# Scores of two local-attention layers in blocks of 64 queries, the tables' load ahead of the weights', and a new order of steps

## The chip, the cores and the metric

The kernel runs on one core of a Trainium2 chip. The metric is the device time of one execution in microseconds; of several runs the median is taken.

## What is computed

Input x has 4 sequences of 1024 tokens with 256 channels, normalised first. Two branches work on it and are added to it: a gated sliding-window attention (16 heads), and two layers of local attention with a gated feed-forward part. The change touches the second branch. A layer of it, cut to what matters (8 heads of 64, window 128, QK_SCALE 8, HID 682):

```python
h = shift_token(x)
q, k, v = jnp.split(h @ wqkv, 3, axis=-1)         # then by heads
q = l2norm(q) * qs
k = l2norm(k) * ksc
q, k = rotary_xpos(q, k)                          # cos, sin and scale tables
sim = jnp.einsum('bhwid,bhwjd->bhwij', bq * 8, bk)  # 128 queries, 256 keys: own and previous block
mask = (i < j) | (i > j + WINDOW) | (j == -1)
attn = jax.nn.softmax(jnp.where(mask, -big, sim), axis=-1)
x = x + o @ wo
h = layernorm(shift_token(x)) * lg + lb
a, g = jnp.split(h @ w1 + b1, 2, axis=-1)
x = x + (a * gelu(g)) @ w2 + b2
```

A query sees its own position and the 128 before it, so 64 neighbouring queries see no more than 192 keys.

## The kernel before

It has two phases. `attention_phase` does the first branch and splits the layers' weights into high and low parts (projections run as three products of such parts). `layers_phase` does the two layers: eight passes (`SEQUENCES`: layer 0 of four sequences, then layer 1 of the same), each in two halves of 512 tokens. What a half does is cut into steps, listed by hand in `ORDER`. Each engine runs through the same list and does its part of each step, so the list sets the order on every engine, SyncE's and ScalarE's DMA queues included; semaphores join the engines. In each half the projections (`transpose_x`, `project_qk`, `rope`, `rope_sum`, `transpose_qk`, `project_v`) already work for the next half, beside attention and feed-forward of this one.

One unit of attention is a pair of heads on two tiles of 128 queries; a half has 8 units:

- `scores` (L1430): TensorE multiplies q and kT for 2 tiles x 2 heads, each 64 rows x 128 queries x 256 keys, into the banks `scores[a % 2][head]`. It waits for `exped` of the unit two before, which frees the bank. `scores` 1 also waits for `out` 1 of the half before, since the feed-forward's sums (`y_banks`) are `scores[1]`. VectorE adds the mask to the scores in place and takes the negative maximum (L1655).
- `softmax` (L1567): ScalarE's exponential with the row's sum. `weigh`: VectorE's reciprocal (L1663), then GpSimd's multiplication (L1305).
- `transpose` (L1438), `values` (L1453), `take_o`, `project_o` (L1352): the weights are transposed, multiplied with the values, and projected.

Other steps: `transpose_x` transposes the next half's x (L1359) into two of the three rotating banks `bank`, ScalarE copies the high part (L1520), VectorE makes the low part of actT (L1606). `project_qk` is 24 records on TensorE, then copies and squares (ScalarE), sums (VectorE, L1611) and a power (GpSimd, L1281). `rope` multiplies by the tables (VectorE L1622 and L1623, GpSimd L1287), `rope_sum` adds (VectorE L1630, L1633). `ln_stats` and `ln_apply` normalise (L1686 to L1709), `transpose_h` transposes (L1368), `up` (L1478, then L1583, L1717, L1587, L1720) and `down` (L1492) are the feed-forward part, `out` adds and stores (L1726, L1256).

SyncE's loads: `load_x` waits for the last transpose of the x before, `load_x1` for the stores of the half before, `load_tables` (L1180) for the last `rope_sum` of the half before. `load_others` does something only at the change of layer: it loads wo (L1183), the rows (L1184), w1 (L1190) and w2 (L1193, L1194) for layer 1. `load_wqkv` loads the projections' weights from ScalarE's queue, in the pass before the change.

Of the kernel before, what the change touches and what calls it, by code (L numbers as in the profile page):

```python
# [24 lines left out]
P = 128  # L25
D = 256
CT = D // P
DH = 64
SEQ = 1024
BATCH = 4  # L30
TILES = 4
# [9 lines left out]
MASKED = -1e30  # L41
# [170 lines left out]
def attention_phase(nc, kept, x, gamma, w_qkv, w_gates, b_gates, w_out, masks, identity, states, attended,  # L212
                    layer_weights, split_weights, tables_in, tables_out, q_scale, k_scale, rows_in, rows_out):

    with ExitStack() as ctx:
# [602 lines left out]
        def _(dve):  # L818
# [120 lines left out]
ORDER = [("scores", 0), ("scores", 1), ("softmax", 0), ("softmax", 1), ("weigh", 0), ("weigh", 1), ("transpose_x", 0), ("load_x", 0),  # L939
         ("scores", 2), ("transpose", 0), ("softmax", 2), ("scores", 3), ("weigh", 2), ("weigh", 3), ("load_x1", 0), ("load_others", 0),  # L940
         ("transpose", 1), ("softmax", 3), ("load_tables", 0), ("project_qk", 0), ("rope", 0), ("scores", 4), ("values", 0), ("values", 1),
         ("take_o", 0), ("transpose", 2), ("project_qk", 1), ("softmax", 4), ("scores", 5), ("weigh", 4), ("transpose", 3), ("rope_sum", 0),
         ("project_qk", 2), ("values", 2), ("softmax", 5), ("scores", 6), ("weigh", 5), ("values", 3), ("rope", 1), ("take_o", 1),
         ("transpose", 4), ("scores", 7), ("softmax", 6), ("transpose_qk", 0), ("weigh", 6), ("project_qk", 3), ("shift_keys", 0),
         ("project_o", 0), ("rope_sum", 1), ("weigh", 7), ("transpose", 5), ("values", 4), ("values", 5), ("softmax", 7), ("take_o", 2),
         ("rope", 2), ("shift_front", 0), ("transpose", 6), ("project_v", 0), ("ln_stats", 0), ("transpose_qk", 1), ("transpose", 7),
         ("ln_apply", 0), ("values", 6), ("values", 7), ("take_o", 3), ("project_v", 2), ("transpose_h", 0), ("project_o", 1), ("rope_sum", 2),
         ("up", 0), ("shift_back", 0), ("up", 1), ("up", 2), ("ln_stats", 1), ("project_v", 1), ("ln_apply", 1), ("down", 0), ("project_v", 3),
         ("up", 3), ("rope", 3), ("x1_bias", 0), ("down", 1), ("down", 2), ("transpose_h", 1), ("load_wqkv", 0), ("up", 4), ("up", 5),
# [5 lines left out]
def layers_phase(nc, kept, attended_end, states, attended, out, wqkv_in, wo_in, w1_in, w2_in, rows_in, tables_in, masks):  # L955
# [3 lines left out]
    with ExitStack() as ctx:  # L959
        def sb(name, shape, dt=F32):  # L960
            return ctx.enter_context(nc.sbuf_tensor(f"f_{name}", shape, dt))

        NU = HALVES * UNITS
        PARTS = 2
        PART = CHUNK // PARTS

        wqkv = layer_projections(kept.weights)
        wo = kept.weights[:, 2 * CT * 3 * F_INNER:KEPT_WEIGHTS].rearrange("p (t c n) -> p t c n", t=2, c=PAIRS)
# [841 lines left out]
```

## Time and profile before

| | |
|---|---|
| median of 3 runs | 2063.93 us (2059.63 to 2064.92) |
| profiled execution | 2062.13 us, span 2060.3 us |
| TensorE matmul busy | 1899.8 us, 92% |
| ScalarE busy | 1400.8 us, 68% |
| VectorE busy | 1324.1 us, 64% |
| GpSimd busy | 959.0 us, 47% |
| mean granted clock of TensorE | 0.986 |
| chain that ended last | TensorE 32%, VectorE 19%, ScalarE 9% of the span |

PE is TensorE, PEld its weight loads, DVE VectorE, ACT ScalarE, POOL GpSimd, SPq SyncE's queue. A float32 matmul stands in the trace as two records, a transpose and an fp32r product as one. A stretch's row gives its ends, its length, and for each engine busy us and the number of records, then the granted clock, the DMA engines' share and GB/s. A timeline's row gives start, length, engine, line, operation, result <- operands, shapes and the number of records merged, and in brackets the engine's idle time before it and what ended it; merged rows overlap at their edges, since the next operation starts before the last one's end. The first transposes of x (L1359) mark the halves' starts: 735.9, 817.7, and so on up to 1906.2 us.

### The profile page before, as it was taken

To read this page: it belongs to the slowest core of one execution; us is meant where nothing else is said; L and a number is where in the kernel's file an instruction comes from. 1 tells how busy PE (TensorE), PEld (TensorE's weight loads), DVE (VectorE), ACT (ScalarE), POOL (GpSimd) and SP (SyncE) were. 2 spreads that over 40 slices of the span, in tenths; PEclk is the share of its full clock that TensorE was granted. 3 is DMA by queue.
4 is the path that set the end of the run, shared out by engine and by line. 5 is a ranking of instruction groups with operands and counts; after the bars stand their busy time and mean duration, and the time that the engine had idled before them with its cause. 6 is when DMAs were issued, how large, how long until landed. Compare 5 with 4: busy or idle time off the path is not lost.

```text
span 2060.3 us, 42560 instructions
## 1 busy us (share of the span) xinstructions
PE 1899.8 (92%) x15184; PEld 1575.3 (76%) x15184; DVE 1324.1 (64%) x4117; ACT 1400.8 (68%) x3933; POOL 959.0 (47%) x1311
## 2 busy tenths in 40 slices
PE   5999999999999789999999999997999999999998
PEld 3777787777777668778788787795877878878777
DVE  4543544444443467777778777775777877877775
ACT  4886977778678465775766757756576575675763
POOL 1532442334234463654736526545264562664732
PEclk9999999999999899999999999998999999999999
DMA  3231322313225411010110110304101011010110
GB/s 126 86 101 43 97 82 78 96 58 89 82 75 161 149 39 36 14 42 11 45 45 12 44 42 15 103 7 158 33 29 52 21 45 55 16 47 22 34 35 26
DMA packets 121493, 121.10 MB, mean 59 GB/s; under 512 B 27188, under 2 KB 100804, under 8 KB 121284
## 3 DMA queue, kind: packets, MB, share of 16 engines
q1 hardware_dynamic: 118116, 112.10, 17.0%
q10 hardware_dynamic: 3168, 6.29, 0.9%
q8 instruction: 122, 2.00, 0.4%
q14 instruction: 87, 0.71, 0.1%
HBM read 72.72 MB, written 37.25 MB: 53 GB/s over the span
## 4 chain that ended last, share of the span: by engine, by line
PE 32%; DVE 19%; ACT 9%; issue 2%; POOL 2%; SPq 1%; DMA 1%; DVEq 0%; ACTq 0%; POOLq 0%
PE f_bank L1352 11%; PE f_scores L1492 4%; ACT f_prob L1567 4%; PE f_scores L1430 4%; DVE f_u L1720 4%; PE f_bank L1478 4%; PE f_bank L1438 3%; DVE f_gu L1717 2%; PE f_o_bank L1453 2%; ACT f_u L1587 2%; DVE y_tok L1703 2%; PE f_bank L1403 2%; DVE y_tok L1709 1%; POOL f_prob L1305 1%; DVE f_sin_part L1623 1%
## 5 line engine op out<-in xcount | busy, mean ns | idle before, releaser
L1305 POOL TENSOR_SCALAR f_prob<-f_prob,f_row_inv 128x256 f32<-128x256 f32 x512 | 263.1, 533 | 331.0 <-DVE f_row_inv L1663 331.0
L568 POOL TENSOR_SCALAR a_prob<-a_prob,a_row_inv,a_gate 128x128 f32<-128x128 f32 x512 | 224.6, 455 | 409.8 <-DVE a_row_inv L898 409.8
L1352 PE MATMUL f_bank<-weights,f_actT 128*128 128x512 f32 x1152 | 305.6, 410 | 1.6 <-DVE f_actT L1606 1.6
L1478 PE MATMUL f_bank<-f_hT,f_w 128*128 128x256 f32 x2112 | 276.5, 286 | 7.7 <-DVE f_gu L1717 7.7
L1478 PEld LDWEIGHTS f_bank<-f_hT,f_w 128*128 128x128 f32 x2112 | 262.1, 190 | 14.3 <-DVE f_gu L1717 10.8
L1567 ACT ACTIVATE f_prob<-f_scores,f_neg_max 128x256 f32<-128x256 f32 x512 | 235.9, 488 | 41.8 <-DVE f_neg_max L1655 40.8
L1352 PEld LDWEIGHTS f_bank<-weights,f_actT 128*128 128x128 f32 x1152 | 211.2, 193 | 51.2 <-ACT f_probT L1514 5.1
L1281 POOL TENSOR_TENSOR f_norm<-f_norm,f_minus_half 128x16 f32<-128x16 f32 x64 | 197.5, 3085 | 24.8 <-DVE f_norm L1615 22.4
L1655 DVE CUSTOM_DVE_ANT_0 f_scores<-f_scores,f_mask 128x256 f32<-128x256 f32 x512 | 199.8, 455 | 13.5 <-PE f_scores L1430 13.4
L1587 ACT ACTIVATE f_u<-f_gu 128x256 fp32r<-128x256 f32 x192 | 80.2, 418 | 180.8 <-DVE f_gu L1717 180.8
L797 ACT ACTIVATE a_prob<-a_scores,a_neg_max 128x128 f32<-128x128 f32 x512 | 179.5, 390 | 30.2 <-DVE a_neg_max L889 28.9
L1287 POOL TENSOR_TENSOR f_qk_tok<-f_qk_tok,tables 128x512 f32<-128x512 f32 x128 | 161.6, 1283 | 71.5 <-DVE f_sin_part L1623 71.5
L591 PE MATMUL a_bank<-a_xT,weights 128*128 128x512 f32 x768 | 191.4, 400 | 0.0
L1438 PE MATMUL f_bank<-ident,f_prob 128*128 128x128 f32 x1024 | 147.8, 280 | 41.9 <-POOL f_prob L1305 15.3
L1720 DVE TENSOR_TENSOR f_u<-f_gu,f_u 128x256 fp32r<-128x256 f32 x192 | 125.6, 654 | 92.9 <-ACT f_u L1587 92.9
L1514 ACT ACTIVATE f_probT<-f_bank 128x512 f32<-128x512 f32 x256 | 146.4, 613 | 54.5 <-PE f_bank L1438 53.5
L591 PEld LDWEIGHTS a_bank<-a_xT,weights 128*128 128x128 f32 x768 | 142.6, 189 | 35.6 <-issue 2.2
L1438 PEld LDWEIGHTS f_bank<-ident,f_prob 128*128 128x128 f32 x1024 | 109.7, 141 | 78.2 <-issue 36.7
L1492 PE MATMUL f_scores<-f_w,f_u 128*128 128x256 f32 (+1 forms) x1152 | 164.2, 286 | 0.0
L1430 PE MATMUL f_scores<-f_kT,f_q 64*128 64x256 f32 x1024 | 147.5, 405 | 17.5 <-ACT f_prob L1567 16.8
L1492 PEld LDWEIGHTS f_scores<-f_w,f_u 128*128 128x128 f32 (+1 forms) x1152 | 148.2, 189 | 6.1 <-issue 2.5
L889 DVE CUSTOM_DVE_ANT_0 a_scores<-a_scores,a_mask 128x128 f32<-128x128 f32 x512 | 129.9, 325 | 34.0 <-PE a_scores L659 34.0
(128 smaller groups left out, 3844.2 us busy)
## 6 DMA issues: line engine op xcount, KB each, us to landing
split_weights<-a_hi_lo SPq DMA_DIRECT2D x16, 512.0 KB, 2.8
x_next<-states SPq DMA_DIRECT2D x32, 256.0 KB, 3.1
tables<-scaled_tables SPq DMA_DIRECT2D x16, 512.0 KB, 6.0
f_x<-states SPq DMA_DIRECT2D x16, 512.0 KB, 5.2
split_weights<-a_hi_lo SPq DMA_DIRECT2D x12, 682.0 KB, 4.0
weights<-split_weights ACTq DMA_DIRECT2D x6, 1024.0 KB, 9.7
f_w<-split_weights SPq DMA_DIRECT2D x4, 1280.0 KB, 9.9
a_x_tok<-in_x SPq DMA_DIRECT2D x8, 512.0 KB, 4.4
```

What stands on the lines that cost most here:

```text
L568: last = nc.gpsimd.tensor_scalar(part, part, row_inv[:, a % 2, head, t:t + 1], gate[:, half, t, h:h + 1], ALU.mult, ALU.mult)
L591: last = nc.tensor.matmul(out, lhs(c, a), rhs(c, b), start=(i == 0), stop=(i == len(order) - 1))
L1281: nc.gpsimd.tensor_tensor(n, n, minus_half[:], ALU.pow).then_inc(norm_ready.sem, 1)
L1305: last = nc.gpsimd.tensor_scalar(part, part, row_inv[:, a % 2, head, t:t + 1], 1.0, ALU.mult, ALU.mult)
L1352: last = nc.tensor.matmul(out, lhs(c, a), rhs(c, b), start=(i == 0), stop=(i == len(order) - 1))
L1430: mm = nc.tensor.matmul(scores[a % 2][head][:, t, :], q[rows, pair, col:col + P], kT[rows, pair, col:col + 2 * P], start=True, stop=True)
L1438: last = nc.tensor.transpose(out[:, j * P:(j + 1) * P], prob[:, a % 2, head, j // 2, (j % 2) * P:(j % 2 + 1) * P], ident[:])
L1478: mm = nc.tensor.matmul(out[:, which * PART:(which + 1) * PART], w1[:, wp, c, col:col + P], hT[:, hp, c, columns_of(a // FH)], start=(i == ...
L1492: mm = nc.tensor.matmul(y_banks[a // FH % PARTS][:, t, :], u[0:m, a % (2 * TILES), up, t * P:(t + 1) * P], w2[0:m, wp, j, :], start=(j == ...
L1567: last = nc.scalar.activation(prob[:, a % 2, head, t, :], scores[a % 2][head][:, t, :], ACT.Exp, bias=neg_max[:, a % 2, head, t:t + 1], sc ...
L1655: last = nc.vector.tensor_tensor_reduce(out=sc, in0=sc, in1=mask[:, min(half * TILES + tile + t, 1)], scale=-1.0, scalar=3e38, op0=ALU.add ...
L1720: nc.vector.tensor_tensor(u[0:m, a % (2 * TILES), LO, :], gu[0:m, a % 2, :], u[0:m, a % (2 * TILES), HI, :].bitcast(F32), ALU.subtract).th ...
```

## The change

1. A `scores` step takes each tile's 128 queries in two blocks of 64 with 192 keys each: 8 matmuls of 64 rows x 64 queries x 192 keys in place of 4 of 64 x 128 x 256. Head 0 and 1 lie in rows 0-63 and 64-127 of the array, block 0 and 1 in columns 0-63 and 64-127. The quarter of the result that isn't written now (block 0's last 64 keys, block 1's first 64) is cleared once, by four memsets at the head of VectorE's part, and TensorE waits for them once before its first scores.
2. Since the mask is added in place over what is left there, its sign and that of q change: the q tables are multiplied by -8, the layers' mask is +1e30 where masked, and VectorE's operation has scale 1.0.
3. `ORDER` is new: `transpose_x` stands between `scores` 0 and 1 and ahead of `softmax` 0; on SyncE the order of the loads is `load_x1`, `load_tables`, `load_x`, `load_others` where it was `load_x`, `load_x1`, `load_others`, `load_tables`; `load_wqkv` stands later; `values`, `transpose_qk`, `rope` 2, `up` and `down` steps are moved.

```diff
-ORDER = [("scores", 0), ("scores", 1), ("softmax", 0), ("softmax", 1), ("weigh", 0), ("weigh", 1), ("transpose_x", 0), ("load_x", 0),
-         ("scores", 2), ("transpose", 0), ("softmax", 2), ("scores", 3), ("weigh", 2), ("weigh", 3), ("load_x1", 0), ("load_others", 0),
-         ("transpose", 1), ("softmax", 3), ("load_tables", 0), ("project_qk", 0), ("rope", 0), ("scores", 4), ("values", 0), ("values", 1),
-         ("take_o", 0), ("transpose", 2), ("project_qk", 1), ("softmax", 4), ("scores", 5), ("weigh", 4), ("transpose", 3), ("rope_sum", 0),
-         ("project_qk", 2), ("values", 2), ("softmax", 5), ("scores", 6), ("weigh", 5), ("values", 3), ("rope", 1), ("take_o", 1),
-         ("transpose", 4), ("scores", 7), ("softmax", 6), ("transpose_qk", 0), ("weigh", 6), ("project_qk", 3), ("shift_keys", 0),
-         ("project_o", 0), ("rope_sum", 1), ("weigh", 7), ("transpose", 5), ("values", 4), ("values", 5), ("softmax", 7), ("take_o", 2),
-         ("rope", 2), ("shift_front", 0), ("transpose", 6), ("project_v", 0), ("ln_stats", 0), ("transpose_qk", 1), ("transpose", 7),
-         ("ln_apply", 0), ("values", 6), ("values", 7), ("take_o", 3), ("project_v", 2), ("transpose_h", 0), ("project_o", 1), ("rope_sum", 2),
-         ("up", 0), ("shift_back", 0), ("up", 1), ("up", 2), ("ln_stats", 1), ("project_v", 1), ("ln_apply", 1), ("down", 0), ("project_v", 3),
-         ("up", 3), ("rope", 3), ("x1_bias", 0), ("down", 1), ("down", 2), ("transpose_h", 1), ("load_wqkv", 0), ("up", 4), ("up", 5),
-         ("down", 3), ("add_attended", 0), ("up", 6), ("up", 7), ("up", 8), ("up", 9), ("rope_sum", 3), ("down", 4), ("transpose_qk", 2),
-         ("down", 5), ("up", 10), ("down", 6), ("up", 11), ("down", 7), ("down", 8), ("transpose_qk", 3), ("out", 0), ("down", 9), ("down", 10),
-         ("down", 11), ("out", 1)]
+ORDER = [("scores", 0), ("transpose_x", 0), ("softmax", 0), ("scores", 1), ("weigh", 0), ("load_x1", 0), ("weigh", 1), ("softmax", 1),
+         ("scores", 2), ("transpose", 0), ("scores", 3), ("weigh", 2), ("softmax", 2), ("load_tables", 0), ("transpose", 1), ("softmax", 3),
+         ("values", 0), ("weigh", 3), ("project_qk", 0), ("values", 1), ("rope", 0), ("load_x", 0), ("scores", 4), ("take_o", 0),
+         ("transpose", 2), ("project_qk", 1), ("scores", 5), ("weigh", 4), ("softmax", 4), ("rope_sum", 0), ("load_others", 0), ("transpose", 3),
+         ("values", 2), ("scores", 6), ("weigh", 5), ("softmax", 5), ("project_qk", 2), ("rope", 1), ("values", 3), ("take_o", 1), ("scores", 7),
+         ("transpose", 4), ("softmax", 6), ("weigh", 6), ("project_qk", 3), ("project_o", 0), ("rope_sum", 1), ("weigh", 7), ("transpose", 5),
+         ("values", 4), ("softmax", 7), ("values", 5), ("take_o", 2), ("transpose", 6), ("project_v", 0), ("transpose_qk", 0),
+         ("shift_front", 0), ("values", 6), ("transpose", 7), ("ln_stats", 0), ("shift_keys", 0), ("ln_apply", 0), ("transpose_qk", 1),
+         ("rope", 2), ("transpose_h", 0), ("values", 7), ("take_o", 3), ("project_v", 2), ("rope_sum", 2), ("up", 0), ("project_o", 1),
+         ("up", 1), ("up", 2), ("project_v", 1), ("shift_back", 0), ("down", 0), ("down", 1), ("ln_stats", 1), ("ln_apply", 1), ("down", 2),
+         ("up", 3), ("project_v", 3), ("rope", 3), ("transpose_h", 1), ("up", 4), ("up", 5), ("down", 3), ("up", 6), ("x1_bias", 0), ("up", 7),
+         ("up", 8), ("down", 4), ("rope_sum", 3), ("down", 5), ("down", 6), ("load_wqkv", 0), ("transpose_qk", 2), ("up", 9), ("up", 10),
+         ("down", 7), ("up", 11), ("down", 8), ("down", 9), ("transpose_qk", 3), ("add_attended", 0), ("out", 0), ("down", 10), ("down", 11),
+         ("out", 1)]
...
+        BLOCK = P // 2
+        KEYS = F_WINDOW + BLOCK
...
+            pe.wait_ge(scores_zeroed, 1)
...
-                            col = (tile + t) * P
-                            for head in (0, 1):
-                                rows = slice(DH * head, DH * (head + 1))
-                                mm = nc.tensor.matmul(scores[a % 2][head][:, t, :], q[rows, pair, col:col + P],
-                                                      kT[rows, pair, col:col + 2 * P], start=True, stop=True)
+                            for b in (0, 1):
+                                col, first = (tile + t) * P + b * BLOCK, b * BLOCK
+                                for head in (0, 1):
+                                    rows = slice(DH * head, DH * (head + 1))
+                                    mm = nc.tensor.matmul(scores[a % 2][head][first:first + BLOCK, t, first:first + KEYS],
+                                                          q[rows, pair, col:col + BLOCK], kT[rows, pair, col:col + KEYS], start=True, stop=True)
...
+            dve.memset(scores[0][0][:], 0.0)
+            dve.memset(scores[0][1][:], 0.0)
+            dve.memset(scores[1][0][:], 0.0)
+            dve.memset(scores[1][1][:], 0.0).then_inc(scores_zeroed, 1)
...
-                                last = nc.vector.tensor_tensor_reduce(out=sc, in0=sc, in1=mask[:, min(half * TILES + tile + t, 1)], scale=-1.0,
+                                last = nc.vector.tensor_tensor_reduce(out=sc, in0=sc, in1=mask[:, min(half * TILES + tile + t, 1)], scale=1.0,
...
-    other = np.where((distance >= 0) & (distance <= window), 0.0, MASKED)
-    first = np.where(first_block & (place < window), MASKED, other)
+    masked = MASKED if window < P else -MASKED
+    other = np.where((distance >= 0) & (distance <= window), 0.0, masked)
+    first = np.where(first_block & (place < window), masked, other)
...
-    tables = np.stack([f(8) * cos * scale, f(8) * sin * scale, cos / scale, sin / scale], axis=1)
+    tables = np.stack([f(-8) * cos * scale, f(-8) * sin * scale, cos / scale, sin / scale], axis=1)
```

## Rows read from the trace of the kernel before

**Rows 1.** Busy time by stretch: two ordinary halves and the change of layer.

```profile
core 0: us, PE busy (x) PEld busy (x) DVE busy (x) ACT busy (x) POOL busy (x), PEclk, DMA share, GB/s
1311.30:1392.80 81.50, 78.42 (x599) 66.41 (x597) 62.27 (x167) 54.88 (x142) 42.46 (x47) 1.00 0.10 30
1392.80:1489.80 97.00, 82.25 (x582) 69.11 (x580) 63.36 (x167) 54.92 (x142) 44.59 (x48) 0.91 0.28 92
1489.80:1572.50 82.70, 78.81 (x598) 66.43 (x596) 63.48 (x167) 54.88 (x142) 44.84 (x48) 1.00 0.11 36
```

**Rows 2.** Waits of TensorE: us in total, times, longest.

```profile
PE f_scores L1430 <- ACT f_prob L1567: 16.8, 16, 2.1
...
PE f_bank L1438 <- DVE f_actT L1606: 12.1, 15, 0.8
...
PE f_bank L1438 <- DVE f_norm L1611: 10.6, 1, 10.6
...
PE f_bank L1478 <- DVE f_gu L1717: 7.7, 15, 0.6
```

**Rows 3.** Timeline of TensorE, one scores step; the middle two are from narrow windows.

```profile
1328.63 1.13 PE L1430 MATMUL f_scores<-f_kT,f_q 64*128 64x256 f32 x8
...
1328.95 0.60 PE L1430 MATMUL f_scores<-f_kT,f_q 64*128 64x256 f32 x4
...
1329.17 0.60 PE L1430 MATMUL f_scores<-f_kT,f_q 64*128 64x256 f32 x4
...
1329.70 1.09 PE L1438 MATMUL f_bank<-ident,f_prob 128*128 128x128 f32 x8
```

**Rows 4.** Timeline of TensorE in the attention phase: two scores steps on quarters.

```profile
533.82 1.98 PE L659 MATMUL a_scores<-a_kT,a_q 64*64 64x128 f32 x64
535.73 4.47 PE L591 MATMUL a_bank<-a_wv,a_xT 128*128 128x512 f32 x18
```

**Rows 5.** Timeline of VectorE at the start of the layers.

```profile
690.00 1.29 DVE L1606 TENSOR_TENSOR f_actT<-f_bank,f_actT 128x512 fp32r<-128x512 f32 x2 [2.49 <-ACT f_actT L1520]
```

**Rows 6.** Timeline of TensorE at the start of a half.

```profile
1311.28 1.09 PE L1359 MATMUL f_bank<-ident,x_next 128*128 128x128 f32 x8
1313.39 1.14 PE L1430 MATMUL f_scores<-f_kT,f_q 64*128 64x256 f32 x8 [1.02 <-ACT f_prob L1567]
1314.97 0.63 PE L1438 MATMUL f_bank<-ident,f_prob 128*128 128x128 f32 x4 [0.45 <-POOL f_prob L1305]
1316.42 0.66 PE L1438 MATMUL f_bank<-ident,f_prob 128*128 128x128 f32 x4 [0.82 <-DVE f_actT L1606]
```

**Rows 7.** Timeline of VectorE there.

```profile
1309.47 0.69 DVE L1726 TENSOR_TENSOR f_x<-f_scores,f_x 128x512 f32<-128x512 f32 x1 [1.27 <-PE f_scores L1492]
1310.50 0.43 DVE L1655 CUSTOM_DVE_ANT_0 f_scores<-f_scores,f_mask 128x256 f32<-128x256 f32 x1 [0.34 <-PE f_scores L1430]
...
1313.52 0.17 DVE L1663 RECIPROCAL f_row_inv<-f_row_sum 128x4 f32<-128x4 f32 x1
```

**Rows 8.** ScalarE there: the timeline, then the chain of waits.

```profile
1308.28 1.28 ACT L1567 ACT_TABLE_LOAD   x1
...
1311.40 3.75 ACT f_prob L1567 x16
```

**Rows 9.** Timeline of GpSimd: the power of one project_qk step.

```profile
1336.98 2.91 POOL L1281 TENSOR_TENSOR f_norm<-f_norm,f_minus_half 128x16 f32<-128x16 f32 x1
```

**Rows 10.** The change of layer: SyncE's timeline, chain, TensorE's timeline, a stretch.

```profile
1411.33 0.36 SPq L1180 DMA_DIRECT2D tables<-scaled_tables  x1
...
1411.33 6.66 DMA tables<-scaled_tables
...
1422.04 1.12 PE L1438 MATMUL f_bank<-ident,f_prob 128*128 128x128 f32 x4 [10.59 <-DVE f_norm L1611]
1422.81 5.28 PE L1352 MATMUL f_bank<-weights,f_actT 128*128 128x512 f32 x12
...
1415.00:1420.00 5.00, 0.00 (x0) 0.00 (x0) 1.99 (x7) 0.00 (x0) 0.62 (x1) 0.50 0.31 99
```

More of the change, by code:

```diff
@@ L1081, in layers_phase @@
         x2_stored = count("x2_stored", {"out": 1}, unit=16, credit=1)
-        pad_zeroed = sem("pad_zeroed")
+        pad_zeroed, scores_zeroed = sem("pad_zeroed"), sem("scores_zeroed")
         consts_loaded = sem("consts_loaded")
```

## The prediction

> **What bounds the kernel now.** The attention phase (the first 689 us) keeps its code, so I read the two layers, which run from 689 us to the end. Their work repeats 16 times, once for each half of each of the eight sequences. I read first the busy time by stretch. A half of layer 0 takes 81.5 us and TensorE is busy for 78.4 of them; a half of layer 1 takes 82.7 us with 78.8. VectorE has 62 to 63 us of work, ScalarE 55, GpSimd 43 to 45 [rows 1]. TensorE's work bounds a half, and the other engines matter where they make it wait. One stretch stands out: the half at the change of layer takes 97.0 us, 14.3 more than its neighbour in layer 1, at a mean granted clock of 0.91 [rows 1].
>
> Second, who made TensorE wait. The 16 waits of scores for the exponentials cost 16.8 us, the 15 of transposes for the low part of actT 12.1, and a single one for f_norm 10.6 [rows 2]. Third, the timelines at the places of these waits: one at the start of each half and one at the change of layer.
>
> **The scores on quarters of the array.** A scores step before is 4 matmuls, 8 records of 256 columns, and the next step starts 1.07 us after it (1329.70 less 1328.63). Its pairs of records start 0.22 us apart (1328.95 and 1329.17), so four pairs make 0.86 and 0.21 lie at the ends of the step [rows 3]. After, a step is 8 matmuls, 16 records of 192 columns, on four quarters. The nearest operation is the attention phase's own: 64 rows on 64 columns, 64 records of 128 columns in two steps, 1.91 us from its start to the next work (535.73 less 533.82) [rows 4]. That is 0.12 us for each group of four; scaled by 192/128 a group takes 0.18 and a new step 0.72 us. This is one bound, a gain of 0.35. The other keeps the 0.21 at the ends whole and scales the four groups by 192/256: 0.65 and 0.21 are 0.86, a gain of 0.21. I take a gain of 0.25, near the second, because the ends of the step stay. There are 128 steps, so TensorE has 32 us less to do (27 to 45), 2.0 us in each half.
>
> Here a rule speaks against the change. The attention phase's records of 128 columns take 1.91/64 = 0.030 us each [rows 4], so a record carries no large fixed price when four run side by side. The Trainium skill, TensorEngine Tiling (Array Packing), Instruction Overhead, gives each matmul some 60 cycles of overhead; with 8 more records in a step that would be an estimated 0.2 us at the full clock, which would leave nearly nothing of the 0.25. By that rule, the sum below would be about 25 us higher; the row disagrees with it, so I don't use it.
>
> The additions of the mask keep their count and shape, only the sign moves to the tables, so they cost what they did. The parts of the scores' banks that no matmul writes any more hold large numbers; their time isn't shown by any row, and I take it as none, since the same instructions read the same number of elements.
>
> **The four memsets.** They stand first on VectorE in the layers, which has to make the low part of actT at 690.0 us, for which it waited 2.49 us [rows 5]. No row shows a memset of these banks by VectorE. By the 0.65 us of each of the two operations in that row (512 columns) four take 2.6 us, and by half of that 1.3; they can start once the engine is in the layers, about 688.5. So TensorE's first projection comes 0 to 1.1 us later. I take 1.0; the lower bound is none.
>
> **The start of a half.** Before, scores 0 and 1 end at 1311.28, the transposes of x follow, and TensorE idles 1.02 us before scores 2, 0.45 before the first four transposes of the weights, 0.82 before the next four: 2.3 us [rows 6]. VectorE subtracts nothing until out 1 has run (1309.47); then two steps of scores last from 1310.50 to 1313.52, 1.5 each [rows 7]. ScalarE loads the table of the exponential at 1308.28 for 1.28 us, under its wait, and then makes 16 exponentials in a row in 3.75, 1.9 for a step [rows 8].
> After, transpose_x stands ahead of softmax 0 and of scores 1. The load stands directly before the first exponential, behind the copies of the step before it [rows 8]; I take it that it stays there. So ScalarE first waits for the transposed x (about 1310.5), copies it twice (0.6 each), loads the table, and begins the exponentials at 1312.9 and not at 1311.4. VectorE does scores 0 to 1311.8, the low part of actT to 1313.1 (two of 0.65), scores 1 to 1314.7, and only then the reciprocal of step 0. GpSimd has the first head at 1315.9, and the transposes of step 0 start at 1316.0 where they began at 1314.97. TensorE idles there some 1 us longer than before, in two waits (before scores 2, and before transpose 0), while the wait for the bank behind actT (0.82) goes. From there I follow the two orders by these durations up to the end of transpose 2: both come out near 1325.9. So four of the eight shortened scores, 1.0 us of the 2.0, are spent at the start of the half.
>
> **The rest of a half.** The other four give 1.0 us. The new order puts rope 2 behind ln_apply 0, which takes two operations (1.3 us) out of the way to transpose_h 0, and it has at most three up steps in a row, where four ended in a wait for VectorE [rows 2] of 0.5 us in a half. Against that, transpose 4 needs weigh 4, which stands on GpSimd behind the power of project_qk 1: one such power is 2.9 us [rows 9], and by my working weigh 4 ends 0.2 us ahead of its use. That is the tightest place; QK 3 also waits some 0.4 for its bank. I take 0.3 us net for the order and give a half 1.3 us (bounds: a loss of 0.5, a gain of 3.0). Over 15 halves that is 19.5 us. The last half has no projections to cover the same chain, and I give it 0.5.
>
> **The change of layer.** Before, SyncE issues the other weights first and the tables only at 1411.33; they land 6.66 us later, and VectorE's rope, and all behind it, waits. TensorE idles 10.59 us, and in that pause the granted clock falls to 0.50, its lower level of 1.2 GHz, so that the next projection's 12 records take 5.28 us [rows 10]. The excess of that half, 14.3 us, is both. After, load_tables stands right behind load_x1 and ahead of load_x and load_others. It is issued near 1396.5 and lands by 1403 with that 6.66, while rope 0 needs it some 15 us after the half's start, about 1407. Who is passed: the load of x for the next half (needed a whole half later) and the other weights. These are issued about 1 us later than before, over 15 us; the first use of wo is 30 us into the half and of w1 45 us. So I take all 14.3 (bounds: 10.6 and 14.5). At the other places the tables were ahead of their use already. The first projections of layer 1 are asked for later, about 20 us ahead of their use; no row makes me charge for it.
>
> **The sum**, against the profiled execution's 2062.1 us (span 2060.3 and 1.8 around it): less 19.5, less 0.5, less 14.3, plus 1.0 gives 2028.8. The median of the runs is 1.8 above the profiled one, so 2030.6; I say **2031**.
>
> **The rivals.**
> - The whole of the gain arrives. The 2.0 us of every half and the start's idle of 2.3 both go, at least by half: 16 x (2.0 + 0.6) + 14.3 - 1 = 55, a time of 2009. For it: TensorE is the fullest engine. Against it: at the start of a half the chain over VectorE, ScalarE and GpSimd has no slack, and two more engines' work is now in it.
> - The chain takes it all. If the start costs 2 us and the rest is bound by VectorE (its row of work in the up steps has hardly a gap), only the change of layer is left: 2064 - 14 + 1 = 2051.
> - The tables still come late, behind x1 and the stores: 2031 + 14 = 2045. Against it, the queue's rows show the wait as issues of the other weights.
> - Slower: weigh 4 falls behind one more power on GpSimd (2.9 us) on top of 1.5 us of ScalarE's copies and table at the start. That is 4.4 us lost in each half against 2.0 saved: 15 x 2.4 = 36 against 14.3, a time of 2087. It decides from a loss of 2.95 us in a half (2.0 + 14.3/15).
> - It doesn't do what it says: the four quarters run two by two. Then a step has eight turns of 0.16 and is 1.5 us, 0.43 more, 128 times: plus 55 on the work, near 2090. The attention phase's 0.12 us for each four speaks against it.
>
> **Chances.** The forecast (2020 to 2040) has 0.58; the whole gain 0.16; the chain takes it all 0.14; tables late 0.04; slower by the chain 0.05; quarters two by two 0.01; and 0.02 for little net effect. For 8 times in 10 the range goes from 2012 to 2050. A measurement of this kernel tells 0.3% (6 us) from no change. Faster by more than that: 0.91; within: 0.03; slower: 0.06.
>
> **What would show it.** Scores steps of 0.80 to 0.86 us from start to next work; a wait before scores 2 of about 3 us and one before transpose 0, but none behind actT; table load behind the copies of actT; no 10 us wait and a clock of 1.00 in the half at the change of layer, which then takes as long as its neighbours; halves of about 80.3 us. I am wrong if scores steps stay above 0.95 us, if GpSimd's weigh 4 or 6 makes TensorE wait in each half, or if w1 or wo comes late.

## The result

The changed kernel takes 2074.8 us (median of 5 runs, 2072.0 to 2078.3) where the kernel before takes 2064.1 on the same chip: a ratio of 1.0059, 95% interval 1.0048 to 1.0070. It is slower by some 11 us; 2031 was forecast, and the range ended at 2050.

| | before | after |
|---|---|---|
| median of the runs | 2064.1 | 2074.8 |
| profiled execution, its span | 2062.1, 2060.3 | 2076.4, 2074.6 |
| mean granted clock of TensorE | 0.986 | 0.971 |
| a half of layer 0 | 81.5 to 82.5 | 83.3 to 84.2 |
| a half of layer 1 | 82.7 to 83.7 | 84.1 to 85.4 |
| the half at the change of layer | 97.0 | 84.5 |

(A half is taken from the start of its transposes of x to the next half's, in the profiled executions.) So the change of layer came out nearly as forecast, and the other halves, forecast to be 1.3 us shorter each, are 1.7 longer on average (84.2 against 82.6). Two halves and one stretch of 2.5 us at the start of the first, in after (the columns are those of [rows 1]):

```profile
1324.50:1407.80 83.30, 78.17 (x664) 66.05 (x660) 61.48 (x164) 55.03 (x142) 44.63 (x47) 0.98 0.10 32
1407.80:1492.30 84.50, 77.94 (x648) 65.27 (x644) 62.64 (x165) 55.07 (x142) 46.88 (x48) 0.98 0.31 104
1330.00:1332.50 2.50, 2.50 (x23) 1.75 (x16) 1.16 (x6) 1.64 (x7) 2.50 (x6) 0.50 1.07 387
```

GpSimd has 2 us more in the half, though it does the same work [rows 1], and a clock of 0.50 appears where it was 1.00. The clock falls so at each of the 14 starts from the second half on, in some only behind scores 2. Who made TensorE wait, in after (us in total, times, longest), beside [rows 2]:

```profile
PE f_scores L1434 <- ACT f_prob L1571: 51.2, 25, 3.2
PE f_bank L1442 <- POOL f_prob L1307: 28.7, 48, 1.2
```

The waits of scores for the exponentials grew from 16.8 us to 51.2. In before the waits of transposes for GpSimd were 15.3.

**The start of a half.** TensorE's timeline in after, to be read against [rows 6]:

```profile
1323.64 0.88 PE L1434 MATMUL f_scores<-f_kT,f_q 64*64 64x192 f32 x16
1324.45 1.09 PE L1361 MATMUL f_bank<-ident,x_next 128*128 128x128 f32 x8
1325.48 0.88 PE L1434 MATMUL f_scores<-f_kT,f_q 64*64 64x192 f32 x16
1329.53 1.56 PE L1434 MATMUL f_scores<-f_kT,f_q 64*64 64x192 f32 x16 [3.17 <-ACT f_prob L1571]
1331.02 1.78 PE L1442 MATMUL f_bank<-ident,f_prob 128*128 128x128 f32 x8
```

and ScalarE's, beside [rows 8]:

```profile
1325.15 1.08 ACT L1524 ACTIVATE f_actT<-f_bank 128x512 fp32r<-128x512 f32 x2 [2.30 <-PE f_bank L1361]
1326.25 1.28 ACT L1571 ACT_TABLE_LOAD   x1
1327.55 0.47 ACT L1571 ACTIVATE f_prob<-f_scores,f_neg_max 128x256 f32<-128x256 f32 x1
```

Scores 0 lasts 0.81 us from its start to the next (1324.45 less 1323.64), as forecast. ScalarE copies, loads its table, and begins the exponentials 3.9 us after scores 0 begins. TensorE waits 3.17 us. What comes next was in no line of the forecast: the granted clock falls to 0.50, the lower level (1.2 GHz), and scores 2 and the transposes behind it take 1.49 and 1.71 us to the next step, where the full clock (2.4 GHz) needs 0.81 and some 1.0.

**The middle of a half.** GpSimd's timeline in after, without a gap from its first power to weigh 7:

```profile
1341.03 3.28 POOL L1283 TENSOR_TENSOR f_norm<-f_norm,f_minus_half 128x16 f32<-128x16 f32 x1 [0.70 <-DVE f_norm L1623]
1344.28 2.51 POOL L1289 TENSOR_TENSOR f_qk_tok<-f_qk_tok,tables 128x512 f32<-128x512 f32 x2
1346.90 2.90 POOL L1283 TENSOR_TENSOR f_norm<-f_norm,f_minus_half 128x16 f32<-128x16 f32 x1
1349.78 5.70 POOL L1307 TENSOR_SCALAR f_prob<-f_prob,f_row_inv 128x256 f32<-128x256 f32 x8
1355.46 2.91 POOL L1283 TENSOR_TENSOR f_norm<-f_norm,f_minus_half 128x16 f32<-128x16 f32 x1
1358.34 2.52 POOL L1289 TENSOR_TENSOR f_qk_tok<-f_qk_tok,tables 128x512 f32<-128x512 f32 x2
1360.84 3.77 POOL L1307 TENSOR_SCALAR f_prob<-f_prob,f_row_inv 128x256 f32<-128x256 f32 x4
1364.57 2.91 POOL L1283 TENSOR_TENSOR f_norm<-f_norm,f_minus_half 128x16 f32<-128x16 f32 x1
1367.47 1.97 POOL L1307 TENSOR_SCALAR f_prob<-f_prob,f_row_inv 128x256 f32<-128x256 f32 x4
```

Weigh 6 (1360.84) takes 3.77 us for four multiplications that take 1.84 elsewhere. TensorE waits for it:

```profile
1364.75 0.63 PE L1442 MATMUL f_bank<-ident,f_prob 128*128 128x128 f32 x4 [1.24 <-POOL f_prob L1307]
```

Why it is slow is seen in narrow windows: two of the multiplications of weigh 6, and what VectorE does at that time (rope_sum 1):

```profile
1361.29 1.44 POOL L1307 TENSOR_SCALAR f_prob<-f_prob,f_row_inv 128x256 f32<-128x256 f32 x1
1362.71 1.44 POOL L1307 TENSOR_SCALAR f_prob<-f_prob,f_row_inv 128x256 f32<-128x256 f32 x1
```

```profile
1360.89 1.50 DVE L1638 TENSOR_TENSOR f_qk_tok<-f_qk_tok,f_sin_part 128x1024 f32<-128x1024 f32 x1 [0.48 <-POOL f_qk_tok L1289]
1362.50 1.31 DVE L1641 TENSOR_TENSOR f_qk_tok<-f_qk_tok,f_norm 128x1024 f32<-128x1024 f32 x1
```

Each of the two starts while one of VectorE's operations on two tiles is running, takes 1.44 us instead of 0.46, and ends 0.34 us behind it (1362.73 against 1362.39, 1364.15 against 1363.81). The whole trace of after has 45 multiplications that start so, three in a half, and every one ends 0.34 to 0.35 us behind VectorE's operation; before has 15, one in a half. The Trainium skill, SBUF — State Buffer, Who interferes with whom, says that a VectorE instruction with two SBUF inputs and a GpSimd one that reads SBUF share a port which one of them holds for its whole instruction, while the other is blocked. By that rule weigh 6 should lose about what is left of the two operations when its multiplications start, 1.10 us each, and the rows agree: 1.93 us in all.

Last, the page's chain that ended last, before and after (shares of the span by engine):

```profile
PE 32%; DVE 19%; ACT 9%; issue 2%; POOL 2%; SPq 1%; DMA 1%; DVEq 0%; ACTq 0%; POOLq 0%
```

```profile
PE 35%; POOL 16%; DVE 7%; ACT 5%; issue 3%; DMA 0%; SPq 0%; ACTq 0%; DVEq 0%; POOLq 0%
```

GpSimd went from 2% to 16%. The chain reaches back to the start of the layers alone (688.7 us in before), which is two thirds of the span. So TensorE, which the forecast made the bound of a half, had about half of it in before, and VectorE more than a quarter.

### The profile page after: what moved, and what is told of

The parts are those of the page before. It is cut to its first block, busy times and chain, and to the rows that moved or that the text cites. A ratio compares the mean times of both kernels' runs of the same rounds, so it can differ in the third digit from the quotient of the medians.

```text
span 2074.6 us, 44612 instructions
## 1 busy us (share of the span) xinstructions
PE 1899.2 (92%) x16208; PEld 1572.8 (76%) x16208; DVE 1301.6 (63%) x4121; ACT 1406.7 (68%) x3933; POOL 985.8 (48%) x1311
## 3 DMA queue, kind: packets, MB, share of 16 engines
q1 hardware_dynamic: 118116, 112.10, 16.8%
## 4 chain that ended last, share of the span: by engine, by line
PE 35%; POOL 16%; DVE 7%; ACT 5%; issue 3%; DMA 0%; SPq 0%; ACTq 0%; DVEq 0%; POOLq 0%
PE f_bank L1482 9%; PE f_bank L1354 9%; POOL f_prob L1307 8%; PE f_scores L1496 6%; POOL f_norm L1283 5%; PE f_bank L1442 3%; PE f_scores L1434 3%; POOL f_qk_tok L1289 2%; PE f_o_bank L1457 2%; DVE f_u L1728 2%; ACT f_prob L1571 2%; PE f_bank L1405 1%; DVE y_tok L1717 1%; ACT L1571 1%; PE f_bank L1370 1%
## 5 line engine op out<-in xcount | busy, mean ns | idle before, releaser
L1307 POOL TENSOR_SCALAR f_prob<-f_prob,f_row_inv 128x256 f32<-128x256 f32 x512 | 294.4, 596 | 336.8 <-DVE f_row_inv L1671 335.8
L1354 PE MATMUL f_bank<-weights,f_actT 128*128 128x512 f32 x1152 | 300.5, 406 | 2.3 <-DVE f_actT L1614 2.3
L1283 POOL TENSOR_TENSOR f_norm<-f_norm,f_minus_half 128x16 f32<-128x16 f32 x64 | 191.9, 2999 | 27.3 <-DVE f_norm L1623 25.6
L1442 PE MATMUL f_bank<-ident,f_prob 128*128 128x128 f32 x1024 | 162.5, 302 | 29.2 <-POOL f_prob L1307 28.7
L1442 PEld LDWEIGHTS f_bank<-ident,f_prob 128*128 128x128 f32 x1024 | 122.2, 153 | 73.7 <-issue 47.3
L1434 PE MATMUL f_scores<-f_kT,f_q 64*64 64x192 f32 x2048 | 128.8, 373 | 52.9 <-ACT f_prob L1571 51.2
L1587 ACT ACTIVATE f_gu<-f_bank,f_rows 128x256 f32<-128x256 f32 x192 | 90.3, 471 | 100.5 <-PE f_bank L1482 99.1
```

The lines of the kernel that those rows point to most:

```text
L1283: nc.gpsimd.tensor_tensor(n, n, minus_half[:], ALU.pow).then_inc(norm_ready.sem, 1)
L1307: last = nc.gpsimd.tensor_scalar(part, part, row_inv[:, a % 2, head, t:t + 1], 1.0, ALU.mult, ALU.mult)
L1354: last = nc.tensor.matmul(out, lhs(c, a), rhs(c, b), start=(i == 0), stop=(i == len(order) - 1))
L1434: mm = nc.tensor.matmul(scores[a % 2][head][first:first + BLOCK, t, first:first + KEYS], q[rows, pair, col:col + BLOCK], kT[rows, pair, co ...
L1442: last = nc.tensor.transpose(out[:, j * P:(j + 1) * P], prob[:, a % 2, head, j // 2, (j % 2) * P:(j % 2 + 1) * P], ident[:])
```

## The experiments

Times are medians; ratios are to the kernel before on the same chip, with 95% intervals. "Old" and "new" name the order of the steps.

### The parts by themselves, and TensorE's clock

**e1**: the old order, with the quarters (scores, mask, memsets); ORDER is that of the kernel before.

```diff
+                            for b in (0, 1):
+                                col, first = (tile + t) * P + b * BLOCK, b * BLOCK
...
+            dve.memset(scores[0][0][:], 0.0)
```

> The kernel before with the quarters, the changed signs and the four memsets, but the old order of steps. Theory A (the new order costs what the quarters give: a wait of 3.2 us at each half's start, after which the clock falls, and a full GpSimd): here the time falls by 10 to 25 us, to about 2046; the scores step is 0.81 us from start to next work, the wait before scores 2 stays under 2 us, the granted clock stays 1.00 there, the change of layer still costs its 14 us. Theory B (the quarters themselves cost: more records, a change of the array's shape at each step): no gain or a loss, 2064 or more, and the work behind a scores step starts later than before.

Measured: 2074.7, ratio 1.0053 (1.0036 to 1.0070). The shorter scores alone make the kernel slower. The time is theory B's, but its reason isn't: a scores step is 0.81 us, and what stands behind it starts no later. Two halves of e1 and a stretch in the second:

```profile
898.50:981.00 82.50, 77.12 (x648) 64.08 (x644) 63.85 (x165) 54.62 (x142) 43.50 (x47) 1.00 0.10 33
1063.60:1147.40 83.80, 79.29 (x649) 66.05 (x645) 62.53 (x165) 54.70 (x142) 43.45 (x47) 0.96 0.11 33
1068.10:1074.90 6.80, 5.98 (x33) 4.61 (x33) 4.50 (x19) 5.47 (x19) 3.23 (x8) 0.50 0.45 148
```

and the same half of the kernel before as the first:

```profile
899.70:982.20 82.50, 78.05 (x582) 65.58 (x580) 63.20 (x167) 54.82 (x142) 43.42 (x47) 1.00 0.10 33
```

Where the clock stays at 1.00 the half takes 82.5 us with either shape: TensorE is busy for 0.9 less and waits 0.9 longer. Read step by step from the half's start, scores 3 to 7 each start 0.22 to 0.28 us later than before, and the step behind each starts when it did, within 0.03 us. In the other half of e1 the clock is at 0.50 for 6.8 us. Around its start TensorE waited three times, the third time as the clock fell:

```profile
1065.90 0.88 PE L1434 MATMUL f_scores<-f_kT,f_q 64*64 64x192 f32 x16 [1.23 <-ACT f_prob L1571]
1067.49 0.63 PE L1442 MATMUL f_bank<-ident,f_prob 128*128 128x128 f32 x4 [0.70 <-POOL f_prob L1307]
1068.94 1.12 PE L1442 MATMUL f_bank<-ident,f_prob 128*128 128x128 f32 x4 [0.82 <-DVE f_actT L1614]
```

2.75 us of waits, where before had 2.29 [rows 6] and kept its clock in every ordinary half. These same waits stand in nearly every start of e1, and a fall follows at 7 of 14.

**e2**: the new order, loads included, with the scores as before.

```diff
-ORDER = [("scores", 0), ("scores", 1), ("softmax", 0), ...
+ORDER = [("scores", 0), ("transpose_x", 0), ("softmax", 0), ("scores", 1), ...
```

> The kernel before with the new order of steps alone; scores stay 64 x 128 x 256. Theory A: the change of layer gives back 12 to 14 us, and each of the other halves loses about 2 to 3.5 us; the sum is 2080 to 2095. TensorE's wait before scores 2 is about 2.7 us. If the clock falls there too, transposes 0 take 1.8 us in place of 1.0. Theory B: faster than before, about 2050.

Measured: 2083.1, 1.0097 (1.0070 to 1.0123). The new order alone is slower by 20 us in spite of its tables. Its halves take 83.4 to 85.6, the one at the change of layer 86.2, TensorE waits 2.92 us ahead of scores 2.

**e3**: the kernel before with the loads moved alone.

```diff
-("transpose_x", 0), ("load_x", 0), ... ("load_x1", 0), ("load_others", 0), ... ("load_tables", 0),
+("transpose_x", 0), ... ("load_x1", 0), ("load_tables", 0), ("load_x", 0), ("load_others", 0), ...
```

> The kernel before with only SyncE's loads moved: load_x1, load_tables, load_x, load_others. All theories: the half at the change of layer takes 83 to 84.5 us in place of 97.0, other halves are unchanged within 0.2 us, and the time is 2050 to 2052. If w1 or wo came late for it, there would be a new wait before the projections of o or the up steps in that half.

Measured: 2052.4, 0.9951 (0.9935 to 0.9967). This part does what it was forecast to do. The half at the change of layer takes 83.7 us, and the clock stays at 1.00 from the first half to the last:

```profile
745.00:1970.00 1225.00, 1163.62 (x8708) 977.47 (x8706) 942.82 (x2430) 813.79 (x2102) 659.98 (x710) 1.00 0.13 40
```

**e4**: e3 with the quarters.

> The quarters of e1 and the loads of e3 with the old order otherwise. Theory A: the two gains add, about 2033 (2025 to 2042). Theory B: no better than e3, 2050 or more.

Measured: 2063.2, 1.0002 (0.9992 to 1.0011): the quarters take 10.8 us of e3's gain away, as theory B had it. Two of its halves:

```profile
983.30:1065.30 82.00, 78.38 (x664) 65.82 (x660) 62.05 (x165) 54.69 (x142) 42.61 (x47) 0.98 0.09 30
1065.30:1149.40 84.10, 79.55 (x649) 66.27 (x645) 62.62 (x165) 54.83 (x142) 43.60 (x47) 0.96 0.10 33
```

The short fall (mean clock 0.98) is made up for within the half (e3 has 82.1 there), the longer one (0.96) costs 1.6 us (82.5 in e3).

**e8**: e4 with the matmuls of scores 1 issued twice.

```diff
+                        for again in range(2 if s == 1 else 1):
```

> e4 (quarters, old order, tables first; 2063.2) with the matmuls of scores 1 done twice, 0.65 us more work for TensorE in a wait of 1.23 us. If e4's 10.8 us above e3 (which has the long scores and no fall of the clock) are the clock's: it stays 1.00 in nearly all halves, and the time is e3's, about 2052 (2049 to 2055), no better, since the shorter scores save nothing in a half whose clock stayed up (82.5 us with and without). If the quarters cost by themselves: 2063 or more.

Measured: 2053.7, 0.9956 (0.9942 to 0.9970), which is e3's time. The repeat fills TensorE's wait (0.58 us ahead of scores 2, where e4 has 1.23), computes nothing new, and 9.5 us come back. So what the quarters cost in the old order is the clock, and the time of the scores themselves is worth nothing there. The clock isn't fully held: it falls for a short time at 5 of e8's 14 starts, where e4 has 8, and that with waits of 2.11 us in all, less than the 2.29 of before. The length of these waits alone doesn't decide it.

### The start of a half in the new order

**e5**: the changed kernel with the matmuls of scores 1 three times over. **e6**: the changed kernel with one exponential of a single column ahead of the copies of x, so that the table is loaded before them. **e7**: both.

```diff
+                    if kind == "transpose_x":
+                        nc.scalar.activation(early[:], ident[:, 0:1], ACT.Exp)
```

> The changed kernel, but the eight matmuls of scores 1 are done three times over (the same result), 1.3 us more work for TensorE in each half, laid into its wait of 3.17 us before scores 2; only the clock can gain by it. If the fall of the clock after that wait costs what the trace shows (scores 2 and the transposes 0 at half speed, about 1.4 us a half in 15 halves): the wait falls to about 1.9 us, the clock stays 1.00 at the halves' starts, and the time falls by 12 to 22 us, to about 2057. If the fall of the clock has another cause, or what it delays is hidden: no gain, 2072 to 2078.

> The changed kernel, but ScalarE makes one exponential of a 128 x 1 column before it waits for the transposed x, so that the table (1.28 us) is loaded in that wait. If the table's load on the chain is what makes the start long: softmax 0 begins some 1.2 us earlier, as soon as VectorE has the first maxima and the copies of actT are done, the wait before scores 2 falls from 3.17 to about 2, the clock stays up, and the time falls to about 2055 (2045 to 2065). If VectorE's order (scores 1 ahead of the reciprocal) holds the start anyway: 2070 or more.

> e5 and e6 together. By the first theory of each, no more than e6 gains plus a few us, about 2052, since both keep the clock up and only e6 shortens the chain. If the rest of a half is held by GpSimd and VectorE, no better than 2048.

Measured: e5 2071.3, 1.0042 (1.0024 to 1.0060); e6 2072.7, 1.0051 (1.0031 to 1.0070); e7 2070.4, 1.0038 (1.0024 to 1.0051). In e5 the wait of 3.17 becomes 1.87 and the clock falls at every second start only. In e6 the wait is split into 1.75 and 1.40 and the clock still falls. In e7 it is 0.45 and 1.84. Each is within 4.4 us of the changed kernel, and the gain of 12 to 22 us that e5's first theory asked for didn't come. The mean granted clock of e5 is 0.985, nearly the 0.986 of before, where the changed kernel has 0.971; so the clock is not where most of its loss lies. The wait of 1.24 us for weigh 6 is in e5 as it was.

### GpSimd's queue

**e9**: the changed kernel with GpSimd's powers taken of 2 of their 16 columns (most of the normalisation of q and k is left out). **e10**: the same in the kernel before.

```diff
-                nc.gpsimd.tensor_tensor(n, n, minus_half[:], ALU.pow).then_inc(norm_ready.sem, 1)
+                nc.gpsimd.tensor_tensor(n[:, 0:2], n[:, 0:2], minus_half[:, 0:2], ALU.pow).then_inc(norm_ready.sem, 1)
```

> The changed kernel with GpSimd's powers (the reciprocal roots of q's and k's sums of squares) taken of 2 of their 16 columns, so that GpSimd spends some 0.4 us instead of 2.9 us on each; the other columns of the normalisation stay sums of squares, so part of the normalisation is left out. GpSimd's theory: in the changed order GpSimd is busy from the first power to weigh 7 without a gap, and TensorE's transposes 6 wait 1.24 us for weigh 6; with the four powers of a half 10 us shorter this wait is gone and what stands behind the powers on VectorE starts earlier, so that a half comes down by 1 us or more: below 2060 us. The rival, that ScalarE's and VectorE's chain with the clock at the start sets a half: the wait of transposes 6 goes, and the time stays within 4 us of the changed kernel's 2075.

> The same short powers in the kernel before, as the control, with the same part of the normalisation left out. GpSimd's theory: GpSimd has 2% of the chain that ended last in the kernel before, so the gain is smaller than the changed kernel's by at least 8 us: 2055 to 2064. The rival: powers are on the chain of both orders alike, and both kernels gain the same.

Measured: e9 2041.9, 0.9895 (0.9875 to 0.9915), 33 us under the changed kernel; e10 2050.0, 0.9930 (0.9904 to 0.9955), 13.5 us under the kernel before. The difference of the gains, some 19 us, is put down to GpSimd's queue in the new order. e10's own number was a miss: an engine with 2% of the chain that ended last was still worth 13.5 us.

**e11**: the changed kernel with one step moved.

```diff
-         ("values", 2), ("scores", 6), ("weigh", 5), ("softmax", 5), ("project_qk", 2), ("rope", 1), ("values", 3), ...
-         ("transpose", 4), ("softmax", 6), ("weigh", 6), ("project_qk", 3), ("project_o", 0), ("rope_sum", 1), ...
+         ("values", 2), ("scores", 6), ("weigh", 5), ("softmax", 5), ("project_qk", 2), ("values", 3), ...
+         ("transpose", 4), ("softmax", 6), ("weigh", 6), ("rope", 1), ("project_qk", 3), ("project_o", 0), ("rope_sum", 1), ...
```

> The changed kernel with one step moved: rope 1 (two multiplications on GpSimd and what feeds them) behind weigh 6 instead of ahead of it, so that weigh 6 doesn't stand behind it and doesn't run beside VectorE's two-input sums. GpSimd's theory: the 1.24 us wait of transposes 6 goes and a half is 1 to 1.5 us shorter: 2055 to 2065. The clock's theory: the clock at the start of a half holds the half, and the middle of it is caught up anyway: within 4 us of 2075.

Measured: 2051.0, 0.9937 (0.9913 to 0.9960). One step moved takes 24 us off the changed kernel, more than was expected. In the profiled executions the ordinary halves average 83.0 us, where the changed kernel has 84.2. GpSimd's timeline in e11:

```profile
1330.93 3.28 POOL L1283 TENSOR_TENSOR f_norm<-f_norm,f_minus_half 128x16 f32<-128x16 f32 x1 [0.71 <-DVE f_norm L1623]
1334.18 2.52 POOL L1289 TENSOR_TENSOR f_qk_tok<-f_qk_tok,tables 128x512 f32<-128x512 f32 x2
1336.81 2.90 POOL L1283 TENSOR_TENSOR f_norm<-f_norm,f_minus_half 128x16 f32<-128x16 f32 x1
1339.70 4.67 POOL L1307 TENSOR_SCALAR f_prob<-f_prob,f_row_inv 128x256 f32<-128x256 f32 x8
1344.34 2.91 POOL L1283 TENSOR_TENSOR f_norm<-f_norm,f_minus_half 128x16 f32<-128x16 f32 x1
1347.24 2.35 POOL L1307 TENSOR_SCALAR f_prob<-f_prob,f_row_inv 128x256 f32<-128x256 f32 x4
1349.56 2.52 POOL L1289 TENSOR_TENSOR f_qk_tok<-f_qk_tok,tables 128x512 f32<-128x512 f32 x2
1352.05 2.90 POOL L1283 TENSOR_TENSOR f_norm<-f_norm,f_minus_half 128x16 f32<-128x16 f32 x1
1354.97 1.84 POOL L1307 TENSOR_SCALAR f_prob<-f_prob,f_row_inv 128x256 f32<-128x256 f32 x4
```

From the first power to the end of weigh 7 it is 25.88 us, where the changed kernel has 28.41; weigh 6 takes 2.35 and not 3.77. These 2.53 us are in the multiplications. But weigh 6 also no longer stands behind rope 1 (2.52 us), so it ends 4.9 us earlier after the first power (18.7 for 23.6), half by the shorter multiplications and half by its place. e11 doesn't tell which half is needed to end the wait of 1.24. The waits of TensorE for weighed scores fall from 28.7 us to 5.1, while those at the starts, and the falls of the clock, are still all there:

```profile
PE f_scores L1434 <- ACT f_prob L1571: 51.1, 25, 3.2
...
PE f_bank L1442 <- POOL f_prob L1307: 5.1, 11, 0.6
```

**e12**: e11 with the matmuls of scores 1 three times over.

> The same, and the matmuls of scores 1 issued three times over, so that TensorE waits shorter for the first exponentials and its clock falls at fewer starts. If both the clock and GpSimd's queue cost time, each by itself, 2048 to 2058, below the kernel before. If neither does, within 4 us of 2071, what the threefold scores 1 gave alone.

Measured: 2042.9, 0.9896 (0.9874 to 0.9918), the fastest kernel that computes all of it: 21 us below the kernel before, and below the expected range. The repeat takes 8.1 us off e11, where it took 3.5 off the changed kernel. That the clock counts for more once GpSimd's queue is out of the way would fit, but the two gains differ by less than their intervals allow to tell.

### What the shape of the scores is worth in the new order

**e13**: e11 with the scores as before. **e14**: e13 with scores 1 issued twice.

> The changed order with rope 1 behind weigh 6, and the scores as before: 128 queries with 256 keys. If the shape of the scores saves nothing and only lowers the clock, this is at or under e11's 2051: 2043 to 2051. If the shorter scores bring part of their 0.25 us a step once GpSimd no longer holds the half, this is slower than e11: 2055 to 2075.

> The same with the matmuls of scores 1 issued twice over, which fills TensorE's wait at the start of a half as the threefold short ones did in e12 (2043). If the shape of the scores is worth nothing: 2040 to 2047. If it is worth its 2 us a half: 2060 to 2075.

Measured: e13 2060.5, 0.9982 (0.9971 to 0.9993); e14 2053.1, 0.9947 (0.9929 to 0.9965). e13 falls into the second case of its expectation, e14 between the two. The shape is worth something here, though not its 2 us a half: 9.4 us between e13 and e11, 10.2 between e14 and e12. It was already worth 8.3 us in the new order with rope 1 at its first place (e2 against the changed kernel). The chains of the pages of e11, e2 and e1:

```profile
PE 47%; ACT 9%; DVE 7%; POOL 1%; issue 1%; DMA 0%; SPq 0%; ACTq 0%; DVEq 0%; POOLq 0%
```

```profile
PE 36%; POOL 15%; DVE 6%; ACT 5%; issue 4%; DMA 0%; SPq 0%; ACTq 0%; DVEq 0%; POOLq 0%
```

```profile
PE 30%; DVE 20%; ACT 10%; POOL 3%; issue 3%; SPq 1%; DMA 0%; DVEq 0%; ACTq 0%; POOLq 0%
```

Of the two thirds of the span that the chain covers, TensorE has most in e11 and less than half in e1. That fits a shape that is worth something in the one and nothing in the other. But e2 has hardly more than the old order, and the quarters gain there as well, so the share doesn't give the price. The runs together:

| order of the steps | scores as before | on quarters |
|---|---|---|
| old | 2064 (before) | 2074.7 (e1) |
| old, tables first | 2052.4 (e3) | 2063.2 (e4) |
| old, tables first, scores 1 twice | | 2053.7 (e8) |
| new | 2083.1 (e2) | 2074.8 (changed kernel) |
| new, rope 1 later | 2060.5 (e13) | 2051.0 (e11) |
| new, rope 1 later, scores 1 repeated | 2053.1 (e14) | 2042.9 (e12) |

## Why the prediction was wrong

The table can be walked from the kernel before to the changed one: 2064, less some 12 for the tables (e3), plus 8 for the rest of the new order with rope 1 later (e13), less 9 for the quarters (e11), plus 24 for rope 1's place (the changed kernel). Such a walk ends at 2075 whatever its steps mean. What the steps are worth shows in other pairs: rope 1's place 22.6 us with the full scores (e2 against e13), the quarters less 8 to 10 in the new order but plus 11 in the old one.

Set against the forecast's terms, the largest part of the 44 us between 2031 and 2075 is GpSimd's. The order was to give 0.3 us in each of 15 halves, 4.5 us, and rope 1's place took 24: 28 us. The shorter scores less what they spend at the start were to give 1.0 us in each half, 15 us, and give about 1 (9 less 8). The change of layer gave 10 to 13 us where 14.3 were forecast.

So three steps failed: every weigh step was taken at the duration of an undisturbed one, shorter scores were taken as time saved because TensorE was taken for the bound, and the wait at the start of a half was charged without the lower clock behind it.

Step by step:

- **"TensorE's work bounds a half."** This failed. The busy share (78.4 of 81.5 us) was read as the bound. But a TensorE whose every step comes just in time is as busy as one that others wait for. e1 and e8 show it: 0.9 us less work in a half and the same 82.5 us, and no gain over e3 where the clock is nearly held. The chain that ended last, with VectorE at 19% beside TensorE's 32%, was a warning and wasn't weighed.
- **A scores step is 0.25 us shorter.** Right (0.81 to 0.82 from start to next, on 1.07). The rule of the Trainium skill, TensorEngine Tiling (Array Packing), Instruction Overhead, on some 60 cycles for each matmul, which the prediction set aside, isn't borne out: by it the step would have gained nearly nothing, and it gained 0.26 us. But 32 us less work for TensorE is worth only 8 to 10 us with the new order and costs 11 with the old one.
- **The memsets, 1.0 us.** Four of 0.48 us; TensorE's first projection waits 2.25 us instead of 1.57, so 0.7 us.
- **The start of a half.** The hand-worked chain was right to some tenths: copies, table, exponentials, a wait of "about 3 us" (3.17), none behind actT. What failed is the step from that wait to its price. The prediction had, in [rows 10], a pause of TensorE followed by a clock of 0.50, and charged the start of a half for the idle time alone. The clock fell at each of the 14 starts, and in the one shown scores 2 and the transposes ran at half speed. Filling the wait gives back 3.5 us in the changed kernel (e5) and 8.1 in e11 (e12).
- **"The tightest place"**: GpSimd was the right engine, the place was weigh 6 in place of weigh 4, and the error lies in a duration: a weigh step, for which the prediction shows no row, was taken at 1.84 us everywhere. The kernel before already shows it at 2.79 where it runs beside rope_sum:

```profile
1334.21 2.79 POOL L1305 TENSOR_SCALAR f_prob<-f_prob,f_row_inv 128x256 f32<-128x256 f32 x4
...
1339.87 1.83 POOL L1305 TENSOR_SCALAR f_prob<-f_prob,f_row_inv 128x256 f32<-128x256 f32 x4
```

  Against the margin of 0.2 us that was stated for weigh 4 this 0.95 is large; in the new order it is 1.93 for weigh 6 and 2.0 for weigh 4 and 5 together. The net gain of 0.3 us from the order was in truth a loss of some 1.6 us a half (24 us over 15 halves). The last section of the prediction named "weigh 4 or 6 makes TensorE wait in each half" as the sign of its error, and that is the row that came.
- **The change of layer, 14.3 us.** Right in kind, somewhat too large: that half is 12.5 us shorter in after and 13.3 in e3, and e3's runs are 10.4 faster.
- **The rivals.** "Slower by the chain" had the engine and the sign, with 0.05. It asked for 4.4 us lost in a half against 2.0 gained. In truth little was gained to begin with, so that 1.7 us lost were enough against the 14.3. That the gain of 2.0 might be worth nothing was only in "the chain takes it all", and no case let it turn into a loss through the clock.

**What stays open.** Why e1, e4 and e8 lose the clock at some starts and not at others, with the same three waits, isn't settled. Nor is how much of rope 1's 24 us is the multiplications beside VectorE's operations and how much is weigh 6's place in GpSimd's queue. Why the quarters gain in the new order, where the clock falls with either shape, and lose in the old one is only partly explained by the clock: with the wait filled they give 10 us in the one (e12 against e14) and nothing in the other (e8 against e3). The attention phase, whose code is the same, varies too: in the profiled executions the layers start at 688.7 us in before, 692.2 in after and 694.5 in e3. That may be why the profiles of before and after differ by 14.3 us and the medians by 10.7, and why e3's gain over the whole is smaller than in its half. The rest of the new order costs 8 us in e13 against e3. Its start is the likely place, since e14's repeat gives 7.4 back, but an order with the old start, the rest of the new one, rope 1 later and the quarters was not tried.

## What to carry over

A high busy share doesn't show that an engine's work is what a shorter step would save: look at what each shortened step lets start earlier. The chain that ended last helps to see which other engines matter, but its shares aren't prices either: GpSimd had 2% in the kernel before, and shorter powers were worth 13.5 us (e10). Where a chain worked out makes TensorE wait longer than any place that keeps its clock, allow for the lower clock in the work behind the wait, and look for a step that could fill it. When steps are reordered, look for what will run side by side on VectorE and GpSimd, and take the duration of a step from the row where it has the same neighbour.

## What the hardware showed

- GpSimd's multiplication of 128x256 takes 0.46 us alone and 1.44 when it starts while VectorE adds or multiplies two tiles of 128x1024. VectorE's is slower as well where GpSimd began first (1.50 against 1.18). Over the run the 512 multiplications take 294.4 us in after, 254.9 in e11.
- Less work on TensorE can cost time: with 0.25 us less in each scores step the three waits at a start grow from 2.29 to 2.76 us, and a granted clock of 0.50 appears there at 8 of 14 starts in e4, where e3 has none. Redundant matmuls of 0.81 us for each half give 9.5 us back (e4 to e8), though with waits of 2.11 us the clock still falls at 5 starts.
- Sixteen records of 64x192 on four quarters take 0.81 us, eight of 64x256 on two halves 1.07.
